# Attention and quantised FFN block on one core: start-up loads cut by halves of partitions over two DMA queues, and the values of batch 0 placed ahead of its query projection

## The reference

```python
x = x + tanh(g_xattn) * xattn(layernorm(x), ctx, ctx, Wq, Wk, Wv)
x = x + tanh(g_ffn)   * ffn(layernorm(x), clip_x, clip_down, w_gate, w_up, w_down)

# xattn: qh = q Wq^T, kh = k Wk^T, vh = v Wv^T
#        scores = qh kh^T / sqrt(256), causal mask, softmax over axis 1 (the queries)
#        out = probs vh
# ffn:   xq = fake_quant(x), one scale from max|x|; weights fake-quantised by rows, I = 704
#        h = fake_quant(silu(xq Wg^T) * (xq Wu^T)), one scale from max|h|; out = h Wd^T
```

## Time and profile before

| | us |
|---|---|
| median of 3 runs | 106.55 (106.26 to 106.69) |
| the profiled execution, its own time | 106.31 |
| its span in the trace | 104.5 |
| PE busy in the span | 96.9 (93%) |
| DVE busy | 80.6 (77%) |
| ACT busy | 66.1 (63%) |
| POOL busy | 43.6 (42%) |
| loads and stores | 13.54 MB in 11176 packets |

### The profile page before, as it was taken

The page is one execution under the profiler, slowest core; times in us unless marked ns, Lnnn a source line. Parts: engine busy times, 40 slices in busy tenths (PEclk is TensorE's granted clock), DMA queues, the critical chain, the costliest instruction groups (busy, mean ns, idle before and its releaser), DMA issues.

```text
span 104.5 us, 1739 instructions
## 1 busy us (share of the span) xinstructions
PE 96.9 (93%) x562; PEld 75.1 (72%) x564; DVE 80.6 (77%) x210; ACT 66.1 (63%) x125; POOL 43.6 (42%) x78
## 2 busy tenths in 40 slices
PE   7799999999999999999999987999999697899990
PEld 2268988988889898897878975444444386889970
DVE  0544296497998999597597979559999998879991
ACT  0421071657972755636738978789888989799800
POOL 6030335047083583508517594055696560350000
PEclk9999999999999999999999999999999999999999
DMA  2999999999354010010985500000000000005555
GB/s 51 333 371 336 376 422 419 419 407 401 138 6 44 0 45 9 23 34 0 150 154 116 110 0 0 0 6 3 0 0 0 0 0 0 0 6 192 209 201 201
DMA packets 11176, 13.54 MB, mean 130 GB/s; under 512 B 6432, under 2 KB 7712, under 8 KB 11168
## 3 DMA queue, kind: packets, MB, share of 16 engines
q1 hardware_dynamic: 10304, 12.39, 37.9%
q10 hardware_dynamic: 864, 1.05, 3.2%
HBM read 10.09 MB, written 2.10 MB: 117 GB/s over the span
## 4 chain that ended last, share of the span: by engine, by line
PE 47%; DVE 20%; DMA 16%; POOL 5%; issue 4%; ACT 3%; SPq 1%; DVEq 0%; POOLq 0%
PE ps L465 9%; DVE hmax L1100 9%; PE ps L686 9%; DMA spread<-rstd 8%; PE ps L503 5%; PE ps L485 5%; DMA r_wide<-spread 5%; DMA wk_sb<-in_wk 4%; DVE shared L1095 4%; PE ps L635 2%; POOL shared L436 2%; PE ps L523 2%; PE ps L540 2%; PE ps L691 2%; PE ps L516 2%
## 5 line engine op out<-in xcount | busy, mean ns | idle before, releaser
L635 PE MATMUL ps<-xq,wguT 128*128 128x512 bf16 x78 | 17.2, 379 | 0.7 <-DVE xq L1075 0.6
L436 POOL TENSOR_TENSOR shared<-up_sb,silu 128x1024 f32<-128x1024 f32 x5 | 11.8, 2366 | 9.5 <-ACT up_sb L830 9.5
L635 PEld LDWEIGHTS ps<-xq,wguT 128*128 128x128 bf16 x80 | 7.8, 98 | 9.8 <-issue 0.6
L465 PE MATMUL ps<-wvT,shared 128*128 128x256 f32 x56 | 13.3, 381 | 0.0
L485 PE MATMUL ps<-shared,a_sb 128*128 128x256 f32 x56 | 13.2, 379 | 0.0
L1100 DVE TENSOR_REDUCE hmax<-shared 128x1 f32<-128x2048 f32 (+1 forms) x6 | 12.7, 2109 | 0.6
L825 ACT ACTIVATE silu<-ps,gu_scale 128x1024 f32<-128x1024 f32 x10 | 11.2, 1115 | 2.1 <-PE ps L635 2.1
L503 PEld LDWEIGHTS ps<-uT,shared 128*128 128x128 f32 x64 | 10.7, 190 | 2.2 <-DVE uT L892 1.0
L503 PE MATMUL ps<-uT,shared 128*128 128x256 f32 (+1 forms) x64 | 12.0, 330 | 0.2 <-DVE uT L892 0.2
L465 PEld LDWEIGHTS ps<-wvT,shared 128*128 128x128 f32 x56 | 10.6, 190 | 1.8 <-DMA shared<-in_xc 0.4
L686 PE MATMUL ps<-hq,wdT 128*128 128x256 bf16 x80 | 10.6, 273 | 0.3 <-DVE hq L1135 0.3
(11 more groups left out here) (120 smaller groups left out, 188.4 us busy)
## 6 DMA issues: line engine op xcount, KB each, us to landing
shared<-in_xc SPq DMA_DIRECT2D x6, 512.0 KB, 10.8
out<-xn SPq DMA_DIRECT2D x7, 256.0 KB, 2.0
xs<-in_x SPq DMA_DIRECT2D x3, 512.0 KB, 8.4
shared<-in_wgu SPq DMA_DIRECT2D x3, 512.0 KB, 7.8
wd<-in_wd SPq DMA_DIRECT2D x1, 896.0 KB, 11.8
shared<-in_xc SPq DMA_DIRECT2D x3, 256.0 KB, 6.9
xs<-in_x ACTq DMA_DIRECT2D x2, 256.0 KB, 5.4
r_wide<-spread SPq DMA_DIRECT2D x4, 128.0 KB, 4.7
```

The lines of the kernel that those rows point to most:

```text
L436: nc.gpsimd.tensor_tensor(hid[:, 2 * i + 1, :], up_sb[i % 2][:], silu1[i % 2][:], ALU.mult).then_inc(hid_done[1], 1)
L465: last = nc.tensor.matmul(values_bank(b, k), ctxT(b)[:, e, k * P:(k + 1) * P], weights[:, e, :], start=(e == 0), stop=(e == KT - 1))
L635: last = nc.tensor.matmul(bank(4 * half + 2 * g + c), wguT[:, i, g, k, :], xq[:, k, col:col + CH], start=(k == 0), stop=(k == KT - 1))
```

## The change

The six loads Wq, Wk, x0, xT(0) and x1 (Wq and xT(0) had been cut by their second index) are now cut by partitions: SP loads partitions 0 to 63 and ACT partitions 64 to 127 of each, 64 rows of 2 KB. Each pair of halves counts on one semaphore, and who waits for it waits for 32. ctxT(0), Wv, xT(1) and ctxT(1) stay whole, and ctxT(1) moves from SP's queue to ACT's. The order on SP is now Wq, Wk, ctxT(0), x0, xT(0), xT(1), x1; on ACT it is Wq, Wk, Wv, x0, xT(0), ctxT(1), x1, scalars.

On PE the second values tile of batch 0 moves ahead of the query projection; the first tile of batch 1 takes its old place ahead of `scores(0)`; `spread_deviation(1)` moves behind `project_queries(1)`. On DVE `stats1(1)` and `variance1(1)` move behind the scaling of batch 0's queries.

```diff
-            sp.dma_start(wq_sb[:, 0], wq_in[:, 0]).then_inc(wq_here[0], 16)
-            sp.dma_start(wk_sb[:], wk_in).then_inc(wk_here, 16)
+            rows = slice(0, P // 2)
+            sp.dma_start(wq_sb[rows], wq_in[rows]).then_inc(wq_here, 16)
+            sp.dma_start(wk_sb[rows], wk_in[rows]).then_inc(wk_here, 16)
             sp.dma_start(ctxT(0), xc_in[0, :, 0]).then_inc(c_here[0], 16)
-            sp.dma_start(xT(0)[:, 0], xc_in[0, :, 1, 0]).then_inc(xT0_here[0], 16)
+            sp.dma_start(xs[rows, 0:QT, :], x[rows, 0:QT, :]).then_inc(x_here[0], 16)
+            sp.dma_start(xT(0)[rows], xc_in[0, rows, 1]).then_inc(xT0_here, 16)
             sp.dma_start(xT(1), xc_in[1, :, 1]).then_inc(xT1_here, 16)
-            sp.dma_start(ctxT(1), xc_in[1, :, 0]).then_inc(c_here[1], 16)
+            sp.dma_start(xs[rows, QT:2 * QT, :], x[rows, QT:2 * QT, :]).then_inc(x_here[1], 16)
             sp.wait_ge(wv_here, 16)
...
             pe.wait_ge(c_here[0], 16)
             pe.wait_ge(wv_here, 16)
-            values_tile(0, 0)
+            for k in range(QT):
+                last = values_tile(0, k)
+            last.then_inc(v_done, 1)
             for f in range(KT):
                 for e in range(KT):
-                    pe.wait_ge(xT0_here[e], 16)
+                    pe.wait_ge(xT0_here, 32)
...
-            values_tile(0, 1).then_inc(v_done, 1)
+            pe.wait_ge(c_here[1], 16)
+            values_tile(1, 0)
 
             for b in range(LAST - 1):
                 scores(b)
+                project_queries(b + 1)
                 if b == 0:
                     spread_deviation(1)
-                project_queries(b + 1)
-                if b == 0:
-                    pe.wait_ge(c_here[1], 16)
-                    values(1)
+                    values_tile(1, 1).then_inc(v_done, 1)
...
-            act.dma_start(wq_sb[:, 1], wq_in[:, 1]).then_inc(wq_here[1], 16)
-            act.dma_start(xs[:, 0:QT, :], x[:, 0:QT, :]).then_inc(x_here[0], 16)
+            rows = slice(P // 2, P)
+            act.dma_start(wq_sb[rows], wq_in[rows]).then_inc(wq_here, 16)
+            act.dma_start(wk_sb[rows], wk_in[rows]).then_inc(wk_here, 16)
             act.dma_start(wvT[:], wvT_in).then_inc(wv_here, 16)
-            act.dma_start(xT(0)[:, 1], xc_in[0, :, 1, 1]).then_inc(xT0_here[1], 16)
-            act.dma_start(xs[:, QT:2 * QT, :], x[:, QT:2 * QT, :]).then_inc(x_here[1], 16)
+            act.dma_start(xs[rows, 0:QT, :], x[rows, 0:QT, :]).then_inc(x_here[0], 16)
+            act.dma_start(xT(0)[rows], xc_in[0, rows, 1]).then_inc(xT0_here, 16)
+            act.dma_start(ctxT(1), xc_in[1, :, 0]).then_inc(c_here[1], 16)
+            act.dma_start(xs[rows, QT:2 * QT, :], x[rows, QT:2 * QT, :]).then_inc(x_here[1], 16)
...
-            for b in range(2):
-                stats1(b)
-                variance1(b)
+            stats1(0)
+            variance1(0)
             for f in range(KT):
                 scale_queries(0, f)
+            stats1(1)
+            variance1(1)
```

More of the change, by code:

```diff
@@ L194, in down_half @@
             return bank2(c - 1)[:, t, :]
-        wq_here = [sem(f"wq_here{h}") for h in range(KT)]
+        wq_here = sem("wq_here")
         wk_here = sem("wk_here")
@@ L202, in gated_block @@
         c_here = [sem(f"c_here{b}") for b in range(2)]
-        xT0_here = [sem(f"xT0_here{e}") for e in range(KT)]
+        xT0_here = sem("xT0_here")
         xT1_here = sem("xT1_here")
@@ L535, in _ @@
             warm_up(WARM_AT_START, AT)
-            pe.wait_ge(wk_here, 16)
+            pe.wait_ge(wk_here, 32)
             for h in range(KT):
@@ L865, in stats1 @@
             def stats1(b):
-                dve.wait_ge(x_here[x_group(b)], 16)
+                dve.wait_ge(x_here[x_group(b)], 32 if b <= 1 else 16)
                 for t in range(QT):
@@ L947, in _ @@
             for h in range(KT):
-                dve.wait_ge(wq_here[h], 16)
+                dve.wait_ge(wq_here, 32)
                 nc.vector.bn_stats(bnq[:, h, :], wq_sb[:, h, :]).then_inc(bnq_done, 1)
```

## The result

| | before | changed |
|---|---|---|
| median | 106.38 us (106.07 to 106.69, 6 runs) | 108.21 us (107.08 to 110.73, 6 runs) |
| ratio | | 1.0135, 95% interval 1.0102 to 1.0168 |
| profiled execution | 106.31 us, span 104.5 | 107.87 us, span 106.1 |

Runs more than 1.5% above the fastest of their kernel are in no ratio of this document, here 108.82 and 110.73, which is why the ratio is less than the 1.017 of the medians; if those two are the change's own doing, the loss is larger. By the ratio the change makes the kernel slower by 1.0 to 1.7%. I had forecast 106.15, "same"; the median lies above my range of 105.6 to 107.7.

A forecast was written before the change was run, and what follows sets the result against it. PE, busy 93% of the span, was taken to bound the kernel. Earlier Wk and Wv, less a 0.39 us wait for x0's rstd, gained 0.4 on 106.31: 105.9, plus 0.24 for the median, 106.15; range 105.6 to 107.7.

The forecast's parts named there:

- the unknown: the pace of a half: Start-up loads: loads filling 64 partitions move at almost full pace; the other end, a pair taking twice its time, stays possible.
- The curve of bytes against time: Start-up loads: landings follow total bytes on both queues, 512 KB per 1.75 to 1.96 us up to 7.36 us.
- Rival (c): Start-up loads: halves of partitions interfere, x0 lands late, a loss of 0.94 us, 107.5; chance 0.30.
- The worst case: Start-up loads: two halves get in each other's way completely, a pair takes twice its time; 108.8 us.
- PE's start: First useful PE product: starts at 4.75 us instead of 5.45, because Wk lands at 4.5.
- The spread: PE ahead of batch 0's deviation spread: waits 0.39 us at 9.13 for rstd, as x0 lands later.
- the term used: Batch 0's statistics up to rstd: 2.11 us, as before, counted from 7.40 to 9.51.
- 0.46 each: ACT's queue: two more DMA issues at 0.46 us each push its table load to about 5.8, ahead of the a_sb copy.
- the work behind `scores(0)`: ACT, DVE and PE up to `attend(0)`: first values at +5.87 us, `attend(0)` at +6.14, first tile about 0.25 ahead, no wait.
- the shift at 11 us: PE around `scores(0)`: equal work at 11.50 instead of 11.89, 0.39 us earlier, arriving at the end in full.
- Rival (d): Attention of batch 0: ACT's later exponentials hold up `attend(0)` and eat the gain, 106.5; chance 0.07.
- my 0.4 us: Whole kernel: the forecast gain, 0.4 us less on the profiled 106.31, so 105.9, or 106.15 as median.

The follow-up runs named there:

- Experiment 10: The changed kernel with its five cut loads cut by second index, now with x0 ahead of ctxT(0) and Wv on both queues: 107.35 us, ratio 1.0073.

## Why the prediction was wrong, step by step

**The step that failed** is the one named "the unknown: the pace of a half". I forecast 106.15, a gain of 0.4; the kernel lost 1.0 to 1.7%. I took almost the full pace "since every row that there is shows both queues moving together"; but all those rows are of loads over 128 partitions, and say nothing on the point. The curve of bytes against time held for the cut by index (Wv and ctxT(0) at 6.84 and 6.64 against 6.4, x0 at 7.73 against 7.36), not for halves: Wk 5.54 for 4.5, Wv 8.93 for 6.4, x0 9.37 for 7.36, xT(0) 10.17 for 8.14. In its place the runs showed 281 to 283 GB/s for 383, and Wk late whenever it came as two loads of 64 rows.

**Rival (c)** happened, to which I gave 0.30. Its mechanism is half of what happened: the range of partitions costs time, shown by the x loads (0.85% there and gone again), at a pace lower by a quarter. Its price, 107.5 at the middle, was 0.7 under the median and 0.3 under the 107.8 of the ratio. That it came so near is luck, since it leaves out two things: the 64-row loads at the start cost by themselves, which no rival of mine had, and Wv, a whole tile, came late with them and held up PE. The worst case, 108.8, by halves that wait for each other completely, was not reached. I had let only halves be slow and only x0 matter.

**PE's start.** Forecast 4.75, was 5.59; the wait for ctxT(0) or Wv, which I had cancelled, grew from 0.40 to 1.16. **The spread.** Forecast 0.39 us of waiting for rstd. In the changed kernel PE did not wait for it: its chain runs through to 11.88, and rstd was there at 11.54, 2.11 us after DVE's start on x0 at 9.43, exactly the term used. The late Wv had taken that wait's place; the 0.18 us ahead of L497 above are of the weight loads alone.

**Issues.** "0.46 each" was too little: the 64-row loads took 0.47 to 0.87, and ACT's table load came at 6.21, not 5.8. It still hid behind PE, but the issues ahead of Wv did not: they are the 0.61 us above, a term that I had put at nothing.

**Right:** the work behind `scores(0)`. `attend(0)` at +6.15 for a forecast +6.14, first values started at +5.38 for +5.45, no wait between, and the shift at 11 us is found again at the end, +1.59 there and +1.6 in the span, though 0.4 of it was gone at 53 us. Rival (d) did not happen.

**The gain that never came.** In the cut by index, where the pace was whole, I should have seen my 0.4 us, and saw none. Wk was there at 4.18, but PE reached the values at 7.35 (7.44 before), not at 6.54. Its chain:

```profile
0.76 4.42 PE ps L456 x10
5.18 2.16 PE ps L541 x8
7.35 1.73 PE ps L466 x8
9.07 0.86 PE ps L554 x4
```

The first line is ten warm-up products, which PE runs while it waits for Wk. They took 4.42 us, and 3.80 in the kernel before:

```profile
0.76 3.80 PE L455 MATMUL ps<-const-bfloat16-1.0 128*128 128x512 bf16 x10 [0.76 <-PEq L1212]
```

Wk and the first `wq_c` were ready before they ended. Then eight instructions took 2.16 us, where L485's eight in the earlier trace rows, by which I had priced them, take 1.73 (0.216 each). Both read as the lower of the clock's two levels lasting longer (1.2 GHz instead of 2.4, 0.43 us for such an instruction): the weight loads of L541 stand 0.43 us apart up to 5.4 us. The granted clock of that stretch reads 1.00, so this rests on the spacing alone. In the run with x by halves the ten took 3.65 us, and the first products came as forecast, values at 6.65:

```profile
4.83 1.98 PE L542 MATMUL ps<-wk_sb,wq_c 128*128 128x256 f32 x8 [0.43 <-DVE wq_c L959]
...
6.65 1.89 PE L467 MATMUL ps<-wvT,shared 128*128 128x256 f32 x8
```

The other half is x0, which landed 0.37 us later than the curve's 7.36. In the cut by index rstd was ready at 9.89 and PE at 9.93:

```profile
9.18 0.71 POOL L378 TENSOR_TENSOR rstd<-var,minus_half 128x2 f32<-128x2 f32 x1
...
10.00 0.19 PEld L496 LDWEIGHTS ps<-ident,rstd 128*128 128x128 f32 x2 [0.47 <-issue]
```

So the 0.4 us do not divide between the two. Each alone held the spread at 9.9, and curing one would have gained nothing. Experiment 10 does not test this cleanly: it brought x0 forward, but made Wv and with it PE late.

**Open:** why Wk is late as two loads of 64 rows, and why it is SP's half; late issues explain half of the cost at most. And by which path the x loads by halves cost their 0.85%, since most of it stood at 53 us in the one profile.

## What to carry to other kernels

Cut a load by an inner index, not by halves of partitions, when two queues share it: the same bytes in the same order were worth 1.4% here. If a forecast rests on a load shape that no row shows, the nearest rows are no evidence for it, and a written rule against it deserves more than the 0.30 that I gave. When loads bound a start-up, a new order pays only if the load that sets the next stage gains and none of the others that it waits for loses.

## What the runs showed of the hardware

As the first loads of their queues, loads of 64 rows took longer to issue than loads of 128 rows with the same bytes, 0.56 to 0.87 us for Wq and Wk against 0.39 to 0.46 by index. It is not the length of the rows: whole loads of 128 rows of 2 KB took 0.40. The whole load of ctxT(0) behind them took 0.58 instead of 0.42, and x0's halves behind that only 0.47.

A late weight can cost more than its lateness. In the second look at the changed kernel PE had been idle 1.13 us for Wk, and its eight instructions then took 3.78 us instead of 1.99, a pace of the lower clock level, though the granted clock reads 1.00:

```profile
6.31 3.78 PE L542 MATMUL ps<-wk_sb,wq_c 128*128 128x256 f32 x8 [1.13 <-DMA wk_sb<-in_wk]
```

In the profile with even and odd partitions everywhere the granted clock itself reads 0.50, after an idle time of 1.87 us:

```profile
6.48 3.01 PE L542 MATMUL ps<-wk_sb,wq_c 128*128 128x256 f32 x8 [1.87 <-DMA wk_sb<-in_wk]
```

```profile
7.00:8.00 1.00, 1.00 (x4) 0.65 0.99 338
8.00:9.00 1.00, 1.00 (x4) 0.50 1.07 404
```

It does not always happen: with Wq and Wk by halves PE waited 1.92 us, and the eight took 1.99. That this is why the changed kernel's six times spread from 107.08 to 110.73, while 22 runs of the loads of before under the same order of work lie between 105.67 and 106.46, is likely, but no run tests it.
